# High parts of the attention's keys and queries: cast by ScalarE between the exponentials instead of by GpSimd

## The reference, cut to what matters

```python
def _L1_xattn_ref(q, k, v, gamma):          # q = layernorm(x), k = v = ctx, 256 rows of 512 a batch
    qh, kh, vh = (a.reshape(B, 8, 32, 512) for a in (q, k, v))
    qk = jnp.einsum('bhdq,bhdl->bhql', qh, kh) * scale
    sm = jax.nn.softmax(qk, axis=-1)
    ret = jnp.einsum('bhql,bhdl->bhdq', sm, vh)
    return gamma * ret.reshape(B, Dv, Lq)
```

## Time and profile before

| | |
|---|---|
| median of 3 runs | 888.57 us (888.16 to 890.78) |
| the profiled execution | 893.75 us, of which 892.0 us is its span |
| busy over the span: PE, DVE, ACT, POOL | 750.1, 582.3, 399.3, 351.3 us |
| mean granted clock of TensorE | 0.932 of full speed |
| head attention, first to last exponential | 391.2 to 652.9 us, 256 exponentials (L1193) |

### The profile page before, as it was taken

The page is one execution under the profiler, slowest core; times in us unless marked ns, Lnnn a source line. Parts: engine busy times, 40 slices in busy tenths (PEclk is TensorE's granted clock), DMA queues, the critical chain, the costliest instruction groups (busy, mean ns, idle before and its releaser), DMA issues. The chain is left out here.

```text
span 892.0 us, 14252 instructions
## 1 busy us (share of the span) xinstructions
PE 750.1 (84%) x4263; PEld 310.0 (35%) x4263; DVE 582.3 (65%) x1086; ACT 399.3 (45%) x741; POOL 351.3 (39%) x352
## 2 busy tenths in 40 slices
PE   3888989559999999859999999999951299999993
PEld 1433443224444444202122222222221155555551
DVE  4668786538585859556888888997646045555552
ACT  1533344126363636137677767767841122222220
POOL 2455554200202021233556568567366023333333
PEclk9999999759999999969899999999985689999998
DMA  7999530050828187223334445443313548889964
GB/s 260 287 126 273 180 122 0 1 174 4 292 70 299 66 313 259 63 72 91 77 96 107 106 122 150 103 131 121 84 61 152 131 84 130 123 128 126 132 95 60
DMA packets 114150, 117.51 MB, mean 132 GB/s; under 512 B 54808, under 2 KB 78232, under 8 KB 113824
## 3 DMA queue, kind: packets, MB, share of 16 engines
q1 hardware_dynamic: 102976, 94.48, 37.2%
q0 software_dynamic: 10384, 22.02, 14.6%
q10 hardware_dynamic: 720, 0.13, 0.1%
HBM read 43.61 MB, written 59.56 MB: 116 GB/s over the span
## 5 line engine op out<-in xcount | busy, mean ns | idle before, releaser
L1193 ACT ACTIVATE l_pt<-l_b 128x512 f32<-128x512 f32 x256 | 139.3, 595 | 54.3 <-PE l_b L1089 42.8
L1704 POOL DMA_INDIRECT out<-ex_y,ex_tag x39 | 61.5, 1576 | 133.1 <-DMA out<-ex_y,ex_tag 56.1
L1600 PE MATMUL ex_hp<-w1h,ex_xt 128*128 x312 | 78.5, 321 | 19.0 <-DMA ex_xt<-slots_x 18.1
L1264 DVE TENSOR_REDUCE l_negm<-l_a 128x2 f32<-128x1024 f32 x64 | 75.3, 1221 | 26.2 <-PE l_a L1034 26.2
L1620 PE MATMUL ex_yp<-w2h,ex_ht 128*128 (+1 forms) x234 | 76.9, 383 | 4.9 <-DVE ex_ht L1664 3.5
L1639 ACT ACTIVATE ex_hf<-ex_pre 128x352 f32<-128x352 f32 x39 | 19.4, 496 | 121.1 <-DVE ex_pre L1659 121.1
L1264 DVE TENSOR_REDUCE h_negm<-l_a 128x2 f32<-128x1024 f32 x56 | 66.0, 1221 | 11.7 <-PE l_a L1034 11.5
L598 PE MATMUL f_gp<-f_xt,wg 128*128 128x512 fp8e4 x256 | 67.4, 387 | 3.8 <-ACT f_y L648 2.7
L1100 PE MATMUL l_pv<-l_pt,l_vt 128*32 128x512 f32 x512 | 69.9, 619 | 0.0
L1108 PE MATMUL l_sm<-l_pt,ones_f 128*32 128x512 f32 x512 | 69.7, 617 | 0.0
L598 PE MATMUL f_up_ps<-f_xt,wg 128*128 128x512 fp8e4 x256 | 67.0, 385 | 0.0
(11 more groups left out here) (245 smaller groups left out, 1486.5 us busy)
## 6 DMA issues: line engine op xcount, KB each, us to landing
slots_x<-empty SPq DMA_DIRECT2D x8, 2376.0 KB, 11.0
slots_x<-empty SPq DMA_DIRECT2D x7, 2112.0 KB, 13.4
h_stack<-h_parts SPq DMA_DIRECT2D x96, 64.0 KB
l_stack<-l_parts SPq DMA_DIRECT2D x96, 64.0 KB
f_stage<-in_w SPq DMA_DIRECT2D x8, 704.0 KB, 4.2
l_ctx<-in_ctx SPq DMA_DIRECT2D x8, 512.0 KB, 7.6
f_stage<-in_w SPq DMA_DIRECT2D x8, 512.0 KB
h_kf<-in_ctx SPq DMA_DIRECT2D x16, 256.0 KB, 3.1
```

What stands on the lines that cost most here:

```text
L1193: act.activation(weights_at(u, c, h)[:, :], B[t % 2][:, :], ACT.Exp, scale=SCALE).then_inc(b_ok, 1)
L1264: dve.tensor_reduce(negm[u % 2][:, 2 * half:2 * half + 2, j], A[half][:, :, :], AX.X, ALU.max, negate=True)\
L1600: mm = pe.matmul(HP[i % 2][:, 0:H], xt[i % AHEAD][:, xp * FC + f, :], w1p[wp][:, bass.ds(e, 1), f * H:(f + 1) * H], start=k == 0, stop=k = ...
L1704: pool.indirect_dma_start(out=out, out_offset=bass.IndirectOffsetOnAxis(ap=tags[i % TAGS][:, 0:1].bitcast(U32), axis=0), in_=y[i % YS][:, ...
```

## The change

The casts of the high parts move from POOL to ACT for all units; POOL keeps the subtractions, which now wait for ACT. ACT casts the queries of unit u + 2 at i = 0 of unit u, after the two exponentials, and the keys of unit u + 3 at i = 6, after the two exponentials and before `high_rows`. The waits that stood ahead of POOL's casts now stand in ACT's order. `F.high_keys` and `F.high_queries` are one ACTIVATE (Copy) each, with a wait for `kf` or `qf` ahead; before, they ran on ACT for units 0 and 1 alone.

```diff
@@ scalar
+            def high_keys(u):
+                act.wait_ge(a_ps, 2 * TC * (u - 1))
+                act.wait_ge(stack_ok[u % 2], STACKED * (u // 2))
+                F.high_keys(act, parts[u % 2], u)
+
             F.high_keys(act, parts[1], 1)
             F.high_queries(act, parts[1], 1)
+            high_keys(2)
             act.wait_ge(ng_ok, 1)
             for u in range(NU):
                 for i in range(CYCLES):
                     weights(u, 2 * i)
                     weights(u, 2 * i + 1)
+                    if i == 0 and u + 2 < NU:
+                        F.high_queries(act, parts[u % 2], u + 2)
+                    if i == 6 and u + 3 < NU:
+                        high_keys(u + 3)
                     if i == ROWS_AT // 2 - 1:
                         mix_out(u)
@@ gpsimd
             def keys(u):
-                if u >= 2:
-                    pool.wait_ge(kf_ok, 16 * u + 16)
-                    pool.wait_ge(a_ps, 2 * TC * (u - 1))
-                    pool.wait_ge(stack_ok[u % 2], STACKED * (u // 2))
-                    pool.tensor_copy(kh[u % 2][:, :], kf[:, :]).then_inc(kh_ok, 1)
                 F.low_keys(pool, parts[u % 2], u)
 
             def queries(u):
-                if u >= 2:
-                    pool.wait_ge(qf_ok, u + 1)
-                    pool.tensor_copy(qh[u % 2][:, :], qf[:, :]).then_inc(qh_ok, 1)
                 F.low_queries(pool, parts[u % 2], u)
```

## The result

The changed kernel takes 935.9 us (median of 4 runs, 930.28 to 937.39), beside 888.37 us for the kernel before in the same runs: 1.0518 times as long, 95% interval 1.0469 to 1.0567. It is 47.5 us slower. The forecast was 935.4 us.

What follows compares the result with a forecast made beforehand. PE was taken to set the pace in head attention. Chain terms of 34.1 us plus 12.7 for clock falls made 46.8, 940.5 us on the profiled execution, 935.4 for the median; range 914 to 952.

Steps and rivals of the forecast that it cites:

- The chain: Late keys' cast at i = 6 delays low_keys, products, normalise, second maximum, qf, queries' cast: 3.70 us per unit.
- T': Start of the next unit's first exponential, 488.00 in the rows; T is the same for the present unit, 472.31.
- What comes back: ACT's idle times for PE at i = 2 and 4 go: 0.43 us returned, leaving 3.27 per plain unit.
- the keys' cast at i = 6: ACT's added cast is covered by waiting for PE: cost zero, at most 7 us if the cover fails.
- Units 7, 8, 11 and 12: Their old stalls swallow part: 2.2 us net in 7 and 11, 2.4 in 8 and 12, 9.2 in all.
- Units 9 and 13: Counted among seven plain units (3, 4, 5, 6, 9, 10, 13) at 3.27 us each, 22.9 in all.
- Units 0 to 2: Late load for unit 3's keys and unit 2's prolonged stall: 2.0 us for the three, bounds 0 to 4.
- The clock: PE's clock falls after the stall in half of eleven units, at 2.3 us: 12.7 us, bounds 0 and 30.
- that rival: The clock falls in all eleven units: 952 us, chance 0.12.
- The port: DVE's normalise and POOL's power exclude each other: 1.37 us instead of 0.69 could add 7.5 us; 0.69 was taken.
- only the queries' wait counts: Rival: later keys find slack on POOL, ACT waits only for qf at i = 0: 12 us, 901 us, chance 0.06.
- POOL's relief wins: Rival: ACT casts keys before POOL would have, subtraction starts sooner: at most 17 us gained, 871 us, chance 0.03.

Runs made afterwards that it cites:

- with the clock kept: Changed kernel with four extra sets of zero-adding matmuls (the filler) on PE in the stall at i = 1, units 3 to 13: 925.74 us, 1.0391.
- the second trace of the same kernel: The changed kernel run again, unaltered, on one chip with the runs of one and four extra sets: 938.95 us, 1.0552.
- one extra set: Changed kernel with one set of zero-adding matmuls on PE in the stall, instead of four: 936.12 us, 1.0508.

## Why the prediction was right

**The chain** was right event by event, to 0.13 us. ACT's idle time ahead of the queries' cast is 3.70 us (about 3.9 forecast), and the exponentials of i = 1 come at T' + 5.32 instead of T + 1.75, 3.57 later (3.70 forecast). That one of these is 3.70 in the forecast and the other in the trace is chance. The runs with one cast each, and the one with POOL's order turned, show that it is a chain and where it can be cut. **What comes back**: 0.43 us was forecast, and 0.34 came (the step from i = 1 to 2 is 1.52 instead of 1.86, that from i = 3 to 4 stays 1.86 with the clock kept); 0.09 for the keys' cast at i = 6 was put at nothing. With the clock kept a plain unit is 3.52 longer, of which 0.20 is the filler's, so 3.3 against the forecast 3.27. **Units 7, 8, 11 and 12** swallowed part of the stall as forecast: with the clock kept they take 2.2 to 2.3 us more each (19.27 against 17.06, 20.46 against 18.12), for 2.2 and 2.4.

**Terms mis-sized.** Units 9 and 13 were counted as plain, but took 17.3 us before, so they lost only 1.8 to 1.9 each with the clock kept, 3 us less in the sum. Units 0 to 2 lost 3.4, not 2.0. **The clock** was right as a mechanism; that its sum was right too is luck, by two errors that cancel. It fell in all eleven units, not in half, so by this the time should have been the 952 us of that rival. But in ten of them the lower level lasted 3.4 us instead of the 6.8 of unit 2 in the kernel before (425.9 to 432.7), and the fall cost 1.7 us in a plain unit and less in the others, not 2.3 to 2.7. Only unit 3 had a fall of 6.8 us, and it cost 2.3, as forecast (21.32 - 19.21, and the filler's 0.20). Units 8 and 12 are 20.5 us long in the changed kernel and with the clock kept, filler included, so there it cost nothing that shows. The sum is 43.6 - 30.4 = 13 us (30.4 being what units 3 to 13 lose with the clock kept and the filler in: 213.8 - 183.4), where 12.7 was forecast; without the filler's 0.20 in each unit, an estimate, it is some 15 us.

**The port.** By the prediction's reading of the rule that it quotes from the Trainium skill, "SBUF — State Buffer", section "Who interferes with whom", `normalise` could have taken 1.37 us in every unit. It took 0.69 in all of units 3 to 13 of the trace after, as at 504.51, where POOL's power on one column (504.37, 0.54 us) was running; so the measurement decides for the shorter price here. Where a POOL operation on 512 columns was running when it started, it did take 1.37: with the queries' cast alone at 475.29, beside a product from 474.95 to 476.11. There the trace agrees with the rule.

**The rivals.** That only the queries' wait counts would have given 901 us; it is out, since taking the keys' cast back to POOL, or its products ahead of it, brings 935.9 down to 897.7 and 901.1. That POOL's relief wins fails at the place named: ACT's slot ends at T' - 2.4. With the keys at i = 5 the slot ends at T' - 5.55, about when POOL's own cast did (T' - 5.7), and nothing is won (1.0021); whether a still earlier slot would give anything was not run, but a plain unit there keeps its 15.69 us, the pace of PE.

That the profiled span grew by 41.2 us and the medians by 47.5 is no contradiction: in the traced execution after the change head attention began 3.9 us earlier (387.33), and what follows unit 13 was 1.9 us shorter. In the second trace of the same kernel head attention began at 391.20, as before the change, and the span is 936.7, 44.7 us more.

## What to carry to other kernels

An operation moved to an engine with idle time must be placed by the moment when its input is there and by the moment when its output is needed, both written against the period of the loop; shares of busy time say neither. Look at what stands behind the consumer in its own engine's order: here two products that had nothing to do with the keys carried the delay to three engines, and turning two lines on POOL took a loss of 5.2% down to 1.2%, while moving the keys' cast by one cycle took the 3.0% that it cost by itself down to 0.2%. A stall that repeats every period costs more than its own length if the clock of TensorE falls after it, here up to 1.7 us a plain unit on top of 3.3.

## What was not expected of the hardware

The falls of the clock settled into the loop: in a plain unit of 20.7 us one fall of 3.4 us follows each stall (489.8 to 493.2 and 510.3 to 513.7), and from unit 7 on all units, whatever they contain, take 20.4 to 20.7 us. The starts of the falls are 20.5 us apart from unit 4 on (469.4, 489.8, 510.3, 530.8 and so on), also while the units still take 20.71. With one extra set, plain units take 20.4 too from unit 4 on. Why the length of a unit locks to the falls was not settled. Much the same idle time of PE wasn't always followed by a fall: in the kernel before, unit 2 with gaps of 1.40 and 0.74 us was, and unit 8 with 1.24 and 0.74 was not, while unit 8 with the same two gaps was when GpSimd's products stood first (clock 0.54 from 522.0 to 525.6). One set of matmuls in the stall kept the clock up in unit 3 alone; filling the stall kept it up in all eleven.
